# A three-layer graph network on one core: the degree chain goes behind the branch, and layer norm's groups are spread through the index chain

## What is computed

```python
h = jnp.maximum(_layernorm(x, axis=-1), 0.0)
deg = segment_sum(ones, dst); inv_deg = 1.0 / jnp.maximum(deg, 1.0)
for l in range(3):                      # "sage" layers
    agg = segment_sum(h[src], dst) * inv_deg
    h = leaky_relu(agg @ Wl.T + b + h @ Wr.T, 0.01)
x = x + h
h = jnp.maximum(_layernorm(x, axis=-1), 0.0)
# one attention layer over the same edges (softmax over each node's edges)
x = x + gat(h @ W, att_src, att_dst, src, dst) + bias
```

## Time and profile before

| | us |
|---|---|
| median of 3 runs | 3276.03 |
| lowest and highest | 3267.15 and 3280.86 |
| the profiled execution, its own time | 3295.59 |
| its span | 3293.9 |
| DVE, PE, POOL, ACT busy in it | 1983.1, 2073.8, 1834.4, 1403.5 |

### The profile page before, as it was taken

How to read it: one execution, slowest core, us unless ns; L and a number is a source line. 1 busy time by engine, 2 the same in 40 slices (tenths; PEclk the granted TensorE clock), 3 DMA queues, 4 the chain that set the end, 5 groups by cost and what they waited for, 6 DMA issues and landing times. The chain is left out here.

```text
span 3293.9 us, 51342 instructions
## 1 busy us (share of the span) xinstructions
PE 2073.8 (63%) x12372; PEld 1809.0 (55%) x12372; DVE 1983.1 (60%) x8287; ACT 1403.5 (43%) x3736; POOL 1834.4 (56%) x1801
## 2 busy tenths in 40 slices
PE   0002677777784776767658989898864444555444
PEld 0001566666673665656547777777754444545444
DVE  7973444444452454544437888888856666666666
ACT  0494233333331222222214555555555555555555
POOL 1003666666646666666646666666635555555553
PEclk9999888899896888878879999999977777777777
DMA  3495566666664666666656777777754444555444
GB/s 98 149 324 170 164 187 197 186 191 189 194 191 114 202 194 192 194 195 199 187 166 188 223 214 219 222 219 220 221 159 118 120 126 123 130 130 126 124 123 111
DMA packets 600937, 576.11 MB, mean 175 GB/s; under 512 B 83405, under 2 KB 561311, under 8 KB 600608
## 3 DMA queue, kind: packets, MB, share of 16 engines
q1 hardware_dynamic: 395104, 311.69, 32.8%
q0 software_dynamic: 57360, 106.10, 14.8%
q10 hardware_dynamic: 148176, 155.01, 13.4%
HBM read 378.74 MB, written 207.75 MB: 178 GB/s over the span
## 5 line engine op out<-in xcount | busy, mean ns | idle before, releaser
L608 POOL DMA_INDIRECT rows<-tab,idx x1323 | 1364.4, 1031 | 880.7 <-issue 355.3
L829 PE MATMUL bank<-mask,rows 128*128 128x128 f32 (+1 forms) x3528 | 707.5, 341 | 160.8 <-issue 129.2
L1233 DVE TENSOR_TENSOR sage<-bank,sage 128x256 f32<-128x256 f32 x588 | 248.4, 423 | 862.8 <-remote 530.2
L829 PEld LDWEIGHTS bank<-mask,rows 128*128 128x128 f32 x3528 | 605.6, 215 | 227.7 <-issue 183.3
L608 POOL DMA_INDIRECT rows<-tab_c,idx x441 | 447.3, 1014 | 430.4 <-PE bank L939 175.8
L701 ACT ACTIVATE sage<-bank,b_col 128x256 f32<-128x256 f32 x392 | 184.9, 472 | 797.2 <-remote 433.5
L1213 DVE TENSOR_SCALAR mask<-iota,dcol 128x256 f32<-128x256 f32 (+1 forms) x1323 | 408.7, 342 | 0.0
L929 PE MATMUL bank<-ident,mask 128*128 128x128 f32 x784 | 171.2, 358 | 376.4 <-ACT mask L761 269.9
L929 PEld LDWEIGHTS bank<-ident,mask 128*128 128x128 f32 x784 | 124.2, 186 | 390.8 <-ACT mask L761 278.1
L781 ACT ACTIVATE sage<-cut_w,ed 128x256 f32<-128x256 bf16 (+1 forms) x441 | 184.7, 472 | 302.4 <-DVE ed L1424 287.4
L854 PE MATMUL bank<-sage,wcat 128*128 128x256 f32 x784 | 268.9, 429 | 50.8 <-issue 45.8
(11 more groups left out here) (212 smaller groups left out, 3476.5 us busy)
## 6 DMA issues: line engine op xcount, KB each, us to landing
sage<-inv_d SPq DMA_DIRECT2D x588, 128.0 KB
turned<-sage ACTq DMA_DIRECT2D x392, 128.0 KB
tab<-sage ACTq DMA_DIRECT2D x392, 128.0 KB
sage<-turned SPq DMA_DIRECT2D x392, 128.0 KB
tab_c<-sage ACTq DMA_DIRECT2D x196, 132.0 KB
own_w<-tab_c SPq DMA_DIRECT2D x196, 132.0 KB
tab<-sage ACTq DMA_DIRECT2D x49, 512.0 KB, 4.4
xin<-tab SPq DMA_DIRECT2D x196, 128.0 KB
```

The costliest lines, as they stand in the source:

```text
L608: eng.indirect_dma_start(out=rows[:, s.win[w], 0:width], out_offset=None, in_=table, in_offset=bass.IndirectOffsetOnAxis(ap=idx[:, s.w + w ...
L829: m = eng.matmul(to[:, a:b], rows[:, s.win[w], 0:D], mask[:, s.mw[w], c:c + b - a], start=(w == 1), stop=(w == 2))
L1233: eng.tensor_tensor(agg_t[:, o.r, :], ps[:, 0:TILE], own_t[:, o.v, :], ALU.add).then_inc(S["sum_v"], 1)
```

## The change

`group_at(g)` changes which rows the g-th group holds: groups 0 to 6 as before, the short one as the eighth (g = 7), and the rest one later. SP loads groups 1 to 4 ahead of the weights instead of group 1 ahead and 2 to 4 behind them. ACT's copies of the weights become a function `weights()` that is called when four groups are through ACT's loop, instead of ahead of it. DVE's groups are spread: two, two, three, two, two between the parts of the index chain, one behind each of the first seven of the eight closing passes, six behind the flag, four while the columns are turned, and the last 20 (29 to 48) at the end. The degree chain leaves this place and is the first thing in `fast_vector`. The split of the bias leaves that place and stands behind the second aggregation stage; PE's wait for `b_v` goes to the same place in PE's program. The store of `deg` to `inv_d` and the wait for it move from POOL's queue (ahead of the branch) to SP's, into the first step of the first stage, behind SP's first six loads of own rows.

```diff
+def group_at(g):
+    return g if g < GR else NSG - 1 if g == GR else g - 1
...
@@ SP, preparation
             load_g(0)
...
-            load_g(1)
+            for g in range(1, GAHEAD):
+                load_g(g)
             wt = S["wt_ld"]
...
-            for g in range(2, GAHEAD):
-                load_g(g)
@@ SP, fast_sync
-            eng.wait_ge(S["inv_st"], 16)
...
+                    if ph == 1 and s.t == 0:
+                        eng.wait_ge(S["deg_v"], 1)
+                        eng.dma_start(inv_d[:, :].rearrange("(u q) e -> u (q e)", q=2),
+                                      deg[:, :, :].rearrange("u q e -> u (q e)")).then_inc(S["inv_st"], 16)
+                        eng.wait_ge(S["inv_st"], 16)
@@ POOL
-            eng.wait_ge(S["deg_v"], 1)
-            eng.dma_start(inv_d[:, :].rearrange("(u q) e -> u (q e)", q=2),
-                          deg[:, :, :].rearrange("u q e -> u (q e)")).then_inc(S["inv_st"], 16)
@@ ACT
             for g in range(NSG + 1):
+                if g == GAHEAD:
+                    weights()
@@ PE, fast_tensor
-            eng.wait_ge(S["b_v"], 1)
...
             eng.wait_ge(S["n_cp"], ka)
+            eng.wait_ge(S["b_v"], 1)
@@ DVE, preparation
-            groups(0, 2)
+            groups(0, 1)
...
+            groups(1, 3)
...
+            groups(3, 5)
...
+            groups(5, 8)
...
+            groups(8, 10)
...
+            groups(10, 12)
...
-            close_up(word, MOVES)
+            for b in range(MOVES):
+                close_up(word, b)
+                if b < MOVES - 1:
+                    groups(12 + b, 13 + b)
...
-            groups(2, 6)
+            groups(19, 25)
...
-            groups(6, 8)
+            groups(25, 29)
...
-            (the degree chain, close_up(ends, MOVES_S) and the reciprocal)
-            groups(8, NSG)
+            groups(29, NSG)
@@ DVE, fast_vector
-            (the split of the bias, 14 instructions)
+            (the degree chain)
...
+            (the split of the bias, behind the two stages' loop)
```

More of the change, by code:

```diff
@@ L618, in scalar_program, with weights @@
         def scalar_program(eng):
[L620 to L626, removed]
             def store_g(g):
                 eng.wait_ge(S["h_a"], g + 1)
-                at = g * SG * TILE
+                at = group_at(g) * SG * TILE
                 eng.dma_start(tab[0][at:at + SG * TILE, :].rearrange("(p j) d -> p (j d)", j=GJ), x_g[:, g % GR, :]
                               ).then_inc(S[f"hg{g % GR}"], 16)
+            def weights():
+                for n in range(7):
+                    eng.wait_ge(S["wt_ps"], n + 1)
+                    to = wcat[:, n // 2, (n % 2) * D:(n % 2 + 1) * D] if n < 6 else w_t[:, :]
+                    eng.activation(to, bank[n][:, 0:P], ACT.Copy).then_inc(S["wt_cp"], 1)
+                eng.activation(wg[:, 0:D], w_raw[:, 6, :], ACT.Copy).then_inc(S["wt_cp"], 1)
+                eng.wait_ge(S["wt_ps"], 8)
+                eng.activation(wg[:, D:D + 2], bank[0][:, 0:2], ACT.Copy).then_inc(S["wg_cp"], 1)
             for g in range(NSG + 1):
+                if g == GAHEAD:
+                    weights()
                 if g < NSG:
@@ L1088, in vector_program, with close_up @@
             eng.sem_inc(S["flag_v"], 1)
+            groups(10, 12)
             op(eng.tensor_copy(fill5[:, :], lead[:, :]))
             op(eng.tensor_tensor(fill5[:, 0:4], lead[:, 0:4], half_n[:, :], ALU.add))
[L1092 to L1099, removed]
[L1100 removed]
+            def close_up(w, b):
+                k = 1 << b
+                op(eng.tensor_scalar(bit[:, :, 0:RUN - k], w[:, :, k:RUN], k, None, ALU.bitwise_and))
+                op(eng.copy_predicated(w[:, :, 0:RUN - k], bit[:, :, 0:RUN - k], w[:, :, k:RUN]))
+            for b in range(MOVES):
+                close_up(word, b)
+                if b < MOVES - 1:
+                    groups(12 + b, 13 + b)
             eng.sem_inc(S["net_v"], 1)
@@ L1190, in shift @@
                                          ALU.mult).then_inc(S["nmr_v"], 1)
[L1192 to L1199, removed]
-            op(eng.scalar_tensor_tensor(b_sum[:, :], b_part[:, 1, :], is_part[:, 1:2], b_sum[:, :], ALU.mult, ALU.add))
-            op(eng.scalar_tensor_tensor(b_sum[:, :], b_part[:, 2, :], is_part[:, 2:3], b_sum[:, :], ALU.mult, ALU.add))
-            op(eng.tensor_copy(b_row[:, 0, :], b_sum[:, :]))
-            eng.tensor_copy(b_row[:, 1, :], b_sum[:, :]).then_inc(S["b_v"], 1)
+            op(eng.tensor_tensor(in_tile[:, :, :], in_tile[:, :, :], valid[:, :, :], ALU.subtract))
+            op(eng.tensor_tensor(w_a[:, :, :], iota[0:HALF, :].unsqueeze(1).to_broadcast([HALF, 2, RUN]),
+                                 drel[:, :, :], ALU.subtract))
+            op(eng.tensor_tensor(ends[:, :, :], w_a[:, :, :], in_tile[:, :, :], ALU.mult))
+            for b in range(MOVES_S):
+                close_up(ends, b)
+            op(eng.tensor_copy(deg[:, :, 0:1], ends[:, :, 0:1]))
+            op(eng.tensor_tensor(deg[:, :, 1:TILE], ends[:, :, 1:TILE], ends[:, :, 0:TILE - 1], ALU.subtract))
+            op(eng.tensor_scalar(deg[:, :, :], deg[:, :, :], 1.0, 1.0, ALU.add, ALU.max))
+            op(eng.reciprocal(deg[:, :, :], deg[:, :, :]))
+            eng.sem_inc(S["deg_v"], 1)
             def masks(g, to, io, done, w, value):
@@ L1266, in fast_vector @@
                 steps(eng, 5, phase)
+            for k in range(SP):
+                op(eng.tensor_scalar(is_part[:, k:k + 1], part[0:SP, 0:1], float(k), None, ALU.is_equal))
+            op(eng.tensor_copy(b_rest[:, 0, :], b_bc[0:SP, LAYERS - 1, :]))
+            for k in range(SP):
+                op(eng.tensor_copy(b_part[:, k, :], b_rest[:, k % 2, :]))
+                if k < SP - 1:
+                    op(eng.tensor_tensor(b_rest[:, (k + 1) % 2, :], b_rest[:, k % 2, :], b_part[:, k, :], ALU.subtract))
+            op(eng.tensor_scalar(b_sum[:, :], b_part[:, 0, :], is_part[:, 0:1], None, ALU.mult))
+            op(eng.scalar_tensor_tensor(b_sum[:, :], b_part[:, 1, :], is_part[:, 1:2], b_sum[:, :], ALU.mult, ALU.add))
+            op(eng.scalar_tensor_tensor(b_sum[:, :], b_part[:, 2, :], is_part[:, 2:3], b_sum[:, :], ALU.mult, ALU.add))
+            op(eng.tensor_copy(b_row[:, 0, :], b_sum[:, :]))
+            eng.tensor_copy(b_row[:, 1, :], b_sum[:, :]).then_inc(S["b_v"], 1)
             for r in range(RING):
```

18 lines of the change are left out of this document (4 added, 14 removed).

## The result

The changed kernel takes 3217.94 us (median of 4 runs, 3215.02 to 3227.57), the kernel before 3275.32 beside it (3267.15 to 3280.86). The ratio is 0.9835, with a 95% interval from 0.9819 to 0.985. That is 57.4 us less by the medians, and 49 to 59 by the interval; forecast were 3220 and 56. The profiled execution took 3219.21 us and its span is 3217.5.

What follows compares the result with a forecast made beforehand. ACT, layer norm's slow engine, stood idle about 90 us in the preparation while DVE ran its chains. Gain 61 less 5 for the degree chain gives 56 off, 3276 to 3220; forecast 3210 to 3229 (0.55), range 3202 to 3245.

Steps and rivals of the forecast that it cites:

- The preparation's sum: Preparation up to POOL's first gather: DVE's pieces in order, last 20 groups at ACT's pace; start about 231, gain 61 us.
- The short group: Layer norm's short group, loaded eighth instead of last: its load lands about when DVE wants it, costing nothing to 2 us.
- The windows: Packed list's windows in the preparation: fetched by 132 us, DVE uses them about 135; just covered, each us later costs one.
- Rival C: Preparation: loads or windows come late and rows of groups wait, 10 to 15 us more; chance 0.27 shared with two rivals.
- The degree chain's cost: First aggregation stage's start, chain moved behind the branch: mostly hidden by POOL's lead; cost 5 us, bounds 0 and 18.
- The lag of the first mean: First stage's start: first mean at about +28 us behind POOL's first gather instead of +9.95, 18 later; POOL's lead hides it.
- Rival B: First stage's start: gathers and degree chain hold each other, 15 to 25 us more, 3235 to 3245; chance 0.27 shared.
- the rule: Trainium skill on DVE and GpSimd sharing SBUF: read as both waiting on each other, so the 18 us lag grows too.
- Rival D: First stage's steady cycle: waits lock otherwise, 2 us more a cycle, kernel slower at 3318; chance 0.03.
- The bias split: Moved to the second stage's end, where DVE waits 6.30 us for stores: costs nothing, 0 to 3.6 if cover is short.

Runs made afterwards that it cites:

- e1: The changed kernel run again without an edit: 3223.2 us, against 3278.4 for the kernel before beside it, ratio 0.9846.
- e3: The changed kernel with the degree chain put back ahead of the branch, ahead of the last 20 groups: 3248.8 us, 25.6 slower than e1.
- e2: The changed kernel without its degree chain, `deg` filled with 0.5 so the means are wrong: 3210.4 us, 12.8 less than e1 by the medians.
- e5: The changed kernel with layer norm's groups where they stood before and ACT's weights first: 2740.2 us, against 2763.2 for the kernel before beside it.
- e6: The changed kernel with the short group last again: 2718.7 us, against 2763.2 for the kernel before beside it.
- e8: The changed kernel with three groups in each closing-up gap instead of one, fewer in later rows: 2703.7 us, against 2763.2 for the kernel before, ratio 0.9782.
- e9: The changed kernel once more without an edit, in the third set: 2712.9 us, against 2765.8 for the kernel before beside it, ratio 0.9809.
- e10: The kernel of e8 again, beside e9: 2704.6 us, 8.3 below e9; ratio to the kernel before 0.9781.
- e7: The kernel before with the short group loaded eighth as the only edit: 2758.1 us, against 2763.2 for the kernel before beside it, ratio 0.9973.
- e4: The changed kernel with nine more closing passes (20.4 us, result unread) in the degree chain behind the branch: 3228.0 us, 4.8 slower than e1.
- e11: The changed kernel with each bit test and predicated copy of the degree chain replaced by three bit tests, degrees wrong: 2707.0 us, 5.8 below e9.

## Why the prediction was right, step by step

- **The preparation's sum.** Right at each point. Row data at 22.99, put down as 22; the windows of the packed list covered (used without a wait); the last 20 groups at 155.54, put down as 155.6 (the row data came 1 us later, and the pacing took about 2 us where 3 were put down); ACT's last square root at 220.23 against 221, and the first gather 9.93 us behind it against 10.05. Gain 61.5 against 61. The sum held because it followed DVE's order piece by piece, with ACT's pace for the last 20 groups only, and took each piece from the trace.
- **The short group.** A wait of 0.34 us within the 0 to 2 given. Its own share, which I didn't name, is 6.5 us at the first gather in the changed kernel and 5.1 in the old one.
- **The windows.** Rival C gave 10 to 15 us for loads or windows that come late. They didn't: DVE's waits for loads of x are 4.3 us in sum over the whole preparation.
- **The degree chain's cost.** I took 5, with bounds 0 and 18. The first stage is longer with the chain in it by 6.2 us (e1 against e3), and by 5 at the second stage's start against e2. In the later sets the five kernels with the chain behind the branch and nothing altered there (e5, e6, e8, e9, e10) have first stages of 609.1 to 612.3 us, and e7, with the chain ahead, 603.7: 5 to 9. So 5 was at the low end of what it is. Single executions wander too: the one of before, with the chain ahead as in e3, has 704.4 us where e3 has 697.1.
- **Its reason was half right, and the 5 is partly luck.** The lag of the first mean, 18 us, is real (+27.95 against +9.95) and POOL's lead takes most of it, as e4 shows. But I took the 5 for what is left of this lag, and left the gathers to a rival with nothing in the sum. e11 shows that the held gathers cost about what they are held, and 7.1 us of hold are enough for the whole 5 to 9: the term had about the right size and came from the other mechanism.
- **Rival B, held gathers.** The mechanism is there and its size was too large. I had 12 to 17 gathers at up to 0.8 us each and as much again on DVE. They are nine, at up to 1.2 us, 7.1 us together; and DVE's chain takes 30.13 us where it took 30.1, so DVE doesn't wait for POOL at all. In the first set only some of the 7.1 reaches the end: without the hold, in e2, POOL waits 2.97 us for TensorE's side ahead of its 35th gather, and in e1 it doesn't. In the third set, where e9 and e11 both have no such wait, 3.3 of the 3.4 us arrive at the 35th gather.
- **What the Trainium skill says on it.** The trace agrees with the Trainium skill (SBUF — State Buffer, "Who interferes with whom") in that a DVE instruction with two inputs in SBUF contends with a GpSimd instruction that reads SBUF: here the gather beside the predicated copy of 235.35 ends 0.97 us behind the copy's end. That both sides would wait, as the prediction took from the rule, isn't seen: the copy of 237.84 starts while that gather is still under way and takes 1.55 us, as it does in the kernel before, where no gather runs (1.54). The Trainium skill says of an instruction with one SBUF input that it stays out of the way unless it runs in a two-port mode; the bit tests of e11 do hold gathers, and at 1278 elements a partition in 0.83 us they are nearly twice as fast for each element as the predicated copy (1278 in 1.58 us), which fits such a mode without proving it; e11 is no test of the second input alone.
- **Rival D, another cycle.** 13.6 us for nine gathers instead of 13.8: nothing locked otherwise. **The bias split** is hidden with 2.72 us to spare.
- **What stays open.** The profiled executions differ by 76 us (3295.6 and 3219.2), the medians by 57. Of the 76, 61.5 are the preparation, 1 the first stage, 9 the second and 6 the third. The change touches the last two only where they meet, by the bias split. e1, the changed kernel again, has 686.7 us in the second stage and 743.9 in the third where the first profile has 681.1 and 746.7, and before 690.0 and 752.3: they wander by some us without an edit, and the profile of before is one execution 20 us over its median. That the median came within 1.4 us of the forecast gain is luck at a spread of this size. And e2's medians give 12.8 us for the chain's presence where its trace gives 5; no run separates these.

## What to carry to other kernels

Where one engine waits for another in a serial preparation, write down both queues and spread the slow engine's independent work through the other's chain, so that the slow engine never stands still for the other; here three groups in each gap did 8 us better than one. Work that the first engine of a stage doesn't need can go behind the stage's start if that engine has a lead over its consumers: 30 us moved, 6 paid. Then look at what the moved work does to the leading engine itself, here the held gathers. An item that loads slowly goes where other work covers its load, not last (5.1 and 6.5 us here).

## What the runs showed of the hardware

A DVE pass on `int32` data in SBUF that runs when an indirect gather starts on POOL holds it until the pass ends: 1.0 us becomes 2.2 beside pairs of a bit test and a predicated copy (a gather every 2.5 us), 1.4 beside bit tests alone (one every 1.7), while DVE's own times stay as they are. Beside the reciprocal on `float32` gathers take 1.00. Which other passes hold a gather, no run sorts out.

The same kernel before took 3278 us in the first set and 2763 in the second; the record has both on the same chip, and the third set, with 2766, on another. The windows of the changed kernel in e1 and then in e9, start of the first stage and its middle:

```profile
260.00:280.00 20.00, 11.45 (x50) 8.54 (x50) 4.39 (x14) 2.03 (x5) 15.42 (x16) 0.81 0.41 118
280.00:300.00 20.00, 11.53 (x49) 10.01 (x50) 8.16 (x26) 4.38 (x11) 12.66 (x13) 0.60 0.36 101
400.00:900.00 500.00, 395.88 (x2040) 342.80 (x2039) 233.73 (x765) 167.35 (x438) 336.55 (x329) 0.87 0.67 192
```

```profile
260.00:280.00 20.00, 19.24 (x120) 17.46 (x120) 16.22 (x52) 8.69 (x23) 15.73 (x15) 1.00 0.75 222
280.00:300.00 20.00, 16.24 (x89) 14.21 (x90) 10.44 (x33) 6.97 (x19) 15.42 (x16) 0.91 0.71 213
400.00:900.00 500.00, 392.64 (x2210) 343.56 (x2211) 271.92 (x846) 176.89 (x462) 374.34 (x364) 0.94 0.73 212
```

From 260 to 300 us the granted clock is 0.81 and 0.60 in e1 and TensorE does 99 matmuls; in e9 it is 1.00 and 0.91 and it does 209. In the middle of the stage it is 2040 against 2210. That bears on a point which puzzled me in the earlier trace rows: in e1, in the changed kernel and before, the fourth and later sums wait up to 12 us with the releaser "remote" just where TensorE's granted clock falls, and in e9 they come every 2 us, with waits under 1 us up to 280, and none over 4 us up to 300. The granted clock is the smaller part of it. TensorE in e1:

```profile
267.94 0.67 PE L861 MATMUL bank<-sage,wcat 128*128 128x256 f32 x2 [1.82 <-issue]
...
272.12 1.94 PE L836 MATMUL bank<-mask,rows 128*128 128x256 f32 x6 [2.86 <-issue]
...
283.44 2.05 PE L836 MATMUL bank<-mask,rows 128*128 128x256 f32 x6 [4.27 <-issue]
290.52 1.19 PE L861 MATMUL bank<-sage,wcat 128*128 128x256 f32 x2 [5.03 <-issue]
```

Six of the sums' matmuls (L836) take 1.04 us at 262.45 and 1.94 to 2.05 here. But TensorE is busy for only 23 of the 40 us (35.5 in e9), of which 17 would be left at e9's mean of 0.17 us for a matmul, and it stands still for up to 5 us at a time with nothing in the profile that it waits for. The first two of these pauses (1.82 and 2.86) come ahead of the first slow matmuls, so the low clock doesn't make them. In the windows of e9 no such pause of TensorE appears, its longest wait there being 2.4 us for a gather. So in the first set it is TensorE's side, with its pauses, that POOL's first stop comes from; what makes the pauses, and how much of the 515 us they, the clock and other things are, no run tells.
